# Layer-norm stage of a fused attention and channel-mix kernel: loads, normalisation and stores in another order, with fewer buffers elsewhere

## What is computed

```python
z   = layernorm(x)                       # over the last axis, eps 1e-5
q, k, v = z @ Wq, z @ Wk, z @ Wv         # 1024 -> 64 each
att = softmax(q @ k.T, axis=1)           # over the queries, not the keys
x1  = x + tile(att @ v, 16)              # 64 columns repeated 16 times
z1  = layernorm(x1)
prev = shift z1 down by one row (first row zero)
xr  = mu_r * z1 + (1 - mu_r) * prev
xk  = mu_k * z1 + (1 - mu_k) * prev
y   = x1 + sigmoid(xr @ W_r.T) * (square(relu(xk @ W_k.T)) @ W_v.T)
```

## Time and profile before

| | us |
|---|---|
| median of 2 runs | 758.27 (753.13 and 763.42) |
| the profiled execution, its own time | 766.0 |
| its span, first to last instruction on its slowest core (core 3) | 764.4 |
| spans of the 8 cores in it | 749.7 to 764.4 |

### The profile page before, as it was taken

The page is one execution under the profiler, slowest core; times in us unless marked ns, Lnnn a source line. Parts: engine busy times, 40 slices in busy tenths (PEclk is TensorE's granted clock), DMA queues, the critical chain, the costliest instruction groups (busy, mean ns, idle before and its releaser), DMA issues.

```text
span 764.4 us, 5687 instructions; the slowest of 8 cores (749.7 to 764.4 us)
## 1 busy us (share of the span) xinstructions
PE 356.5 (47%) x1392; PEld 125.2 (16%) x1392; DVE 310.8 (41%) x531; ACT 244.0 (32%) x420; POOL 47.7 (6%) x77
## 2 busy tenths in 40 slices
PE   0001300000995887777772000000237999999875
PEld 0000100000440111111112000000012444444332
DVE  3540532425751111111112586626891002227777
ACT  3202204004007888888870231210003233330000
POOL 2110111102000030000000010100000000001110
PEclk9999855555995556666655555555567999999998
DMA  9647575593701059920000004494200000007764
GB/s 237 191 166 110 165 206 80 204 218 116 110 1 33 8 72 170 234 90 2 1 0 1 14 27 144 158 212 87 44 0 0 1 1 0 1 1 249 236 231 165
DMA packets 77854, 76.22 MB, mean 100 GB/s; under 512 B 60189, under 2 KB 60205, under 8 KB 77758
## 3 DMA queue, kind: packets, MB, share of 16 engines
q0 software_dynamic: 13504, 32.32, 16.0%
q1 hardware_dynamic: 12606, 30.68, 12.5%
q10 hardware_dynamic: 51712, 12.85, 10.4%
HBM read 47.79 MB, written 21.76 MB: 91 GB/s over the span
## 4 chain that ended last, share of the span: by engine, by line
PE 27%; DMA 22%; DVE 18%; issue 15%; ACT 9%; ACTq 7%; DVEq 1%; SPq 1%; POOL 0%; POOLq 0%
DMA xst<-x_in 8%; PE ktp L886 7%; PE rps L844 7%; ACT p_sb L552 6%; PE dpool L492 6%; ACTq L314 5%; DMA z1T<-z1dram 4%; DMA zdram<-zst 4%; DMA y_out<-x2b 3%; DVE x1b L683 3%; DVE xk L823 2%; DVE tmp L993 2%; DVE tmp L989 2%; DVE zst L355 2%; PE dpool L473 2%
## 5 line engine op out<-in xcount | busy, mean ns | idle before, releaser
L552 ACT ACTIVATE p_sb<-dpool,negm 128x1024 bf16<-128x1024 f32 x128 | 140.6, 1124 | 22.2 <-DVE negm L517 20.7
L844 PE MATMUL rps<-wrT,xr 128*128 128x512 bf16 x256 | 60.2, 401 | 157.7 <-DVE xr L814 138.7
L492 PE MATMUL dpool<-qrep,krep 64*128 64x512 bf16 x256 | 101.0, 562 | 42.7 <-ACT p_sb L552 38.1
L392 PE MATMUL qk<-zT,wqk 128*128 128x512 bf16 x64 | 18.3, 439 | 181.6 <-DVE qrep L423 108.0
L944 PE MATMUL ops<-wvT,kaT 128*128 128x512 bf16 x256 | 59.6, 395 | 8.9 <-DVE tmp L989 7.1
L301 ACT ACTIVATE junk<-xst 128x1024 bf16<-128x1024 f32 x32 | 33.8, 1057 | 91.5 <-issue 83.8
L367 DVE TENSOR_REDUCE sums<-xst 128x1 f32<-128x1024 f32 x32 | 39.0, 1220 | 55.1 <-DMA xst<-x_in 55.0
L523 DVE TENSOR_REDUCE ell<-ellp 128x1 f32<-128x4 f32 x32 | 5.0, 157 | 134.6 <-ACT p_sb L552 134.5
L844 PEld LDWEIGHTS rps<-wrT,xr 128*128 128x128 bf16 x256 | 26.0, 102 | 191.6 <-issue 164.6
L886 PE MATMUL ktp<-xk,wkT 128*128 128x512 bf16 x256 | 55.6, 379 | 1.7 <-ACT r_sb L857 1.3
L911 DVE TENSOR_TENSOR kaT<-krl 128x512 bf16<-128x512 bf16 x32 | 13.6, 425 | 98.3 <-ACT krl L902 98.2
(11 more groups left out here) (83 smaller groups left out, 385.7 us busy)
## 6 DMA issues: line engine op xcount, KB each, us to landing
xst<-x_in SPq DMA_DIRECT2D x32, 512.0 KB, 8.6
xst<-x_in POOLq DMA_DIRECT2D x32, 512.0 KB, 6.6
zdram<-zst POOLq DMA_DIRECT2D x32, 256.0 KB, 8.7
y_out<-x2b SPq DMA_DIRECT2D x16, 512.0 KB, 3.6
z1dram<-z1b SPq DMA_DIRECT2D x16, 256.0 KB, 2.9
wrT<-wrT_in POOLq DMA_DIRECT2D x1, 2048.0 KB, 18.5
wkT<-wkT_in POOLq DMA_DIRECT2D x1, 2048.0 KB, 30.5
wvT<-wvT_in POOLq DMA_DIRECT2D x1, 2048.0 KB, 42.5
```

The source lines that it names most:

```text
L392: t.matmul(qk[buf][:, :], wqk[:, ct * 128:(ct + 1) * 128], zT[ct][:, nch * 512:(nch + 1) * 512], start=(ct == 0), stop=(ct == CT - 1), ski ...
L492: t.matmul(units[u][:, cc * 512:(cc + 1) * 512], krep[64 * a:64 * (a + 1), kt * 128:(kt + 1) * 128], qrep[64 * a:64 * (a + 1), c * 512:(c ...
L552: sc.activation(p_sb[kt % 4][:, s * 1024:(s + 1) * 1024], units[u][:, :], AF.Exp, bias=negm[:, kt:kt + 1], accum_out=ellp[:, 4 * (kt % 2) + s:
L844: ins = t.matmul(r_ps[t_ % 2][:, hh * 512:(hh + 1) * 512], xr[ct][:, t_ * 128:(t_ + 1) * 128], wrT[:, ct * C + hh * 512:ct * C + (hh + 1) ...
```

## The change

1. Stage A's order on DVE: the sums of group 0 come first; then for g = 1 to 7 the statistics and applies of group g - 1, and after them the sums of group g. A planner of its own, `plan_ln_af`, writes the counts. Stage F keeps the old one.
2. `zst` has 8 slots instead of 4. The apply of tile i waits for the store of tile i - 8, and ACT's squares are written into the same slot of `zst` that the apply fills later, so that the square of tile i too waits for the store of tile i - 8. `junk` is gone; so is `rowb`, whose three rows lie in `zst`.
3. `vs_sb` is `v_sb` (scaled in place), `krl` is gone (relu goes into `kaT` and is squared in place), `p_sb1` lies in the space that `zT` has left.
4. `z1dram` has 2080 rows instead of 2176: 15 and 16 zero rows instead of 63 and 64. The 16 transposes take 1040 rows instead of 1088, and H reads `z1T` from columns 16 and 15 instead of 64 and 63.

The diff, cut to its core:

```diff
-    z1dram = nc.dram_tensor("z1dram", [2176, C], BF16).ap()
+    z1dram = nc.dram_tensor("z1dram", [2080, C], BF16).ap()
-        zst = e(nc.sbuf_tensor("zst", [128, 4 * C], BF16))
-        junk = e(nc.sbuf_tensor("junk", [128, C], BF16))
+        zst = e(nc.sbuf_tensor("zst", [128, 8 * C], BF16))
...
+        vs_sb = v_sb
...
+        def plan_ln_af(n_tiles, sv0):
...
+            for s4 in range(4):
+                sv += 1
+                cnt[("sum", s4)] = sv
+            for g in range(1, ng + 1):
+                gm = g - 1
+                for op in ("smean", "svar", "msq", "varsub", "recip", "nmr"):
+                    sv += 1
+                    cnt[(op, gm)] = sv
+                for s4 in range(4):
+                    sv += 1
+                    cnt[("apply", 4 * gm + s4)] = sv
+                if g < ng:
+                    for s4 in range(4):
+                        sv += 1
+                        cnt[("sum", 4 * g + s4)] = sv
...
-        a_za = lambda i: 16 * (i // 4 + 1)
+        a_za = lambda i: 16 * (i // 8 + 1)
...
+                    if i >= 8:
+                        sc.wait_ge(ZAs[i % 8], a_za(i - 8))
...
-                    sc.activation(junk[:, :], xst[:, (i % 8) * C:(i % 8 + 1) * C],
+                    sc.activation(zst[:, (i % 8) * C:(i % 8 + 1) * C],
+                                  xst[:, (i % 8) * C:(i % 8 + 1) * C],
                                   AF.Square,
...
-                    for s in range(4):
-                        sc.wait_ge(ZAs[s], 16 * (2 * qtr + 2))
+                    for s in range(8):
+                        sc.wait_ge(ZAs[s], 16 * (qtr + 1))
...
-                    if i >= 4:
-                        v.wait_ge(ZAs[i % 4], a_za(i - 4))
+                    if i >= 8:
+                        v.wait_ge(ZAs[i % 8], a_za(i - 8))
...
-            for g in range(8):
+            def a_sums_emit(v, g):
...
+            a_sums_emit(v, 0)
+            for g in range(1, 8):
+                emit_ln_fin(v, g - 1, A_CNT, a_square(4 * (g - 1) + 3),
+                            a_sqrt(g - 1))
+                a_apply_emit(v, g - 1)
+                a_sums_emit(v, g)
...
-                sc.dma_start(out=z1T[ctn][:, 0:1088],
-                             in_=z1dram[0:1088, ctn * 128:(ctn + 1) * 128],
+                sc.dma_start(out=z1T[ctn][:, 0:1040],
+                             in_=z1dram[0:1040, ctn * 128:(ctn + 1) * 128],
...
-                v.tensor_scalar(xr[ct][:, :], z1T[ct][:, 64:2112],
+                v.tensor_scalar(xr[ct][:, :], z1T[ct][:, 16:2064],
...
-                    sc.activation(krl[:, tc * 512:(tc + 1) * 512],
+                    sc.activation(kaT[dt][:, tc * 512:(tc + 1) * 512],
```

More of the change, by code:

```diff
@@ L86, in build_program @@
         rowf = e(nc.sbuf_tensor("rowf", [128, C], F32))
-        rowb = e(nc.sbuf_tensor("rowb", [128, C], BF16))
         xlast = rowf[0:1, :]
         x1x = rowf[32:33, :]
-        z1x = rowb[0:1, :]
-        z1xm = rowb[32:33, :]
-        jrow = rowb[64:65, :]
+        z1x = zst[0:1, C:2 * C]
+        z1xm = zst[32:33, C:2 * C]
+        jrow = zst[64:65, C:2 * C]
         outx_row = e(nc.sbuf_tensor("outx_row", [1, D], F32))
@@ L108, in build_program @@
             nc.sbuf_tensor("v_sb", [128, KT * D], BF16),
-            nc.sbuf_tensor("vs_sb", [128, KT * D], BF16),
             nc.sbuf_tensor("p_sb0", [128, S], BF16),
-            nc.sbuf_tensor("p_sb1", [128, S], BF16),
             nc.sbuf_tensor("negm", [128, KT], F32),
@@ L116, in build_program @@
         ]
-        (qrep, krep, v_sb, vs_sb, p_sb0, p_sb1, negm, ellp, ell, rell) = opens(attn_cm)
+        (qrep, krep, v_sb, p_sb0, negm, ellp, ell, rell) = opens(attn_cm)
+        vs_sb = v_sb
         vT_sb = p_sb0
-        p_sb = [p_sb0, p_sb1]
+        p_sb = [p_sb0]
         SW = e(nc.semaphore("SW"))
@@ L447, in build_program @@
         out_tok, = opens(out_cm)
-        z1T_cm = [nc.sbuf_tensor(f"z1T{i}", [128, 2176], BF16, side="right") for i in range(CT)]
+        z1T_cm = [nc.sbuf_tensor(f"z1T{i}", [128, 2080], BF16, side="right") for i in range(CT)]
         z1T = opens(z1T_cm)
@@ L455, in build_program @@
         out_sb, outx_sb, xp_sb = opens(out2_cm)
-        cm_p23 = [nc.sbuf_tensor("p_sb2", [128, S], BF16, side="right"),
+        cm_p23 = [nc.sbuf_tensor("p_sb1", [128, S], BF16, side="right"),
+                  nc.sbuf_tensor("p_sb2", [128, S], BF16, side="right"),
                   nc.sbuf_tensor("p_sb3", [128, S], BF16, side="right")]
@@ L660, in _ @@
             sy.wait_ge(SD, sd_row63 - 16)
-            sy.dma_start(out=z1dram[63:64, :], in_=z1xm).then_inc(SD, 16)
+            sy.dma_start(out=z1dram[15:16, :], in_=z1xm).then_inc(SD, 16)
             sy.wait_ge(SV, SV_F0 + 11)
             sy.wait_ge(SD, sd_zero1 - 16)
-            sy.dma_start(out=z1dram[0:63, :],
-                         in_=bass.AP(zst, 0, [[4 * C, 63], [1, C]])).then_inc(SD, 16)
+            sy.dma_start(out=z1dram[0:15, :],
+                         in_=bass.AP(zst, 0, [[8 * C, 15], [1, C]])).then_inc(SD, 16)
             sy.wait_ge(SD, sd_zero2 - 16)
-            sy.dma_start(out=z1dram[2112:2176, :],
-                         in_=bass.AP(zst, 0, [[4 * C, 64], [1, C]])).then_inc(SD, 16)
+            sy.dma_start(out=z1dram[2064:2080, :],
+                         in_=bass.AP(zst, 0, [[8 * C, 16], [1, C]])).then_inc(SD, 16)
             for g in range(4):
@@ L672, in _ @@
                     sy.wait_ge(SV, F_CNT[("apply", t_)])
-                    sy.dma_start(out=z1dram[64 + t_ * 128:64 + (t_ + 1) * 128, :],
+                    sy.dma_start(out=z1dram[16 + t_ * 128:16 + (t_ + 1) * 128, :],
                                  in_=z1b[:, s * C:(s + 1) * C]).then_inc(ZSs[s], 16)
@@ L758, in _ @@
                         sc.wait_ge(SV, F_CNT[("svar", g - 2)])
-                    sc.activation(junk[:, :], x1b[:, (t_ % 8) * C:(t_ % 8 + 1) * C],
+                    sc.activation(zst[:, 2 * C:3 * C], x1b[:, (t_ % 8) * C:(t_ % 8 + 1) * C],
                                   AF.Square,
@@ L782, in _ @@
                 sc.wait_ge(SG_HI, 16 * ctn)
-                sc.dma_start(out=z1T[ctn][:, 1088:2176],
-                             in_=z1dram[1088:2176, ctn * 128:(ctn + 1) * 128],
+                sc.dma_start(out=z1T[ctn][:, 1040:2080],
+                             in_=z1dram[1040:2080, ctn * 128:(ctn + 1) * 128],
                              transpose=True).then_inc(SG_HI, 16)
@@ L911, in _ @@
                     v.tensor_tensor(kaT[dt][:, tc * 512:(tc + 1) * 512],
-                                    krl[:, tc * 512:(tc + 1) * 512],
-                                    krl[:, tc * 512:(tc + 1) * 512],
+                                    kaT[dt][:, tc * 512:(tc + 1) * 512],
+                                    kaT[dt][:, tc * 512:(tc + 1) * 512],
                                     ALU.mult).then_inc(SV, 1)
         closes(cm_ktp)
-        closes(krl_cm)
         closes(xk_cm)
```

24 lines of the change are left out of this document (11 added, 13 removed).

## The result

The changed kernel takes 743.7 us at the median of 11 runs; the kernel before, 762.2 at the median of 10. The ratio is 0.9754, with a 95% interval of 0.9713 to 0.9795: faster, by 18.4 us at the medians. 739 was forecast, with a range of 731 to 750. With eight more runs the median of the kernel before rose from 758.3 to 762.2, so the 19 us that were taken off it came out closer than the time itself.

A forecast was written before the change was run, and what follows sets the result against it. Stage A was taken as bound by a loop of waits, not one resource. On core 3, 13.0 + 5.5 + 5.5 - 3.3 + 1.0 = 21.7 us; 19 off the 758.3 median gave 739, range 731 to 750.

The forecast's parts named there:

- First quarter, 13.0: Stage A, core 3: group 1's applies 15.5 us earlier, but DMA work frees ACT at 58.4 instead of 71.4: 13.0 gained.
- Second and third quarter, 5.5 each: Stage A: applies 9.8 us apart instead of 16.55, 6.7 gained, 1.2 taken back for leftover loads beside stores: 5.5 each.
- the wait chain ends last: Stage A, second and third quarter: waits, not DMA work (34.0 us against 43.0 used), set the end; 6.7 gained before deduction.
- Last quarter, 3.3 lost: Stage A: group 7's sums, formerly hidden by transposes, now stand between the applies: 9.8 us instead of 6.6, 3.3 lost.
- The waits on stores, nothing: Stage A: ACT's squares waiting for the store of tile i - 8 add nothing; eight slots keep the 15.5 us whole.
- z1dram and H, 1.0: Second-round transposes, 48 rows of 1088 fewer: between nothing and 2.3 us for 16 of them, 1.0 us gain taken.
- The rest at nothing: Squares into zst, vs_sb in place, p_sb1 moved, relu and square within kaT: same instructions at other addresses, no time.
- From core 3 to the median: Whole kernel: gains of 21.7 us on core 3 and 18.0 on core 5 taken as 19 off the median.
- the slowed streams: Rival, stage A: denser loads and stores run at 209 GB/s instead of 290, gain 9.4 us, 749; chance 0.18.
- the waits go whole (731): Rival, stage A: stores land as before, leftover loads delay no transposes, gain 27.9 us, 730.4; chance 0.10.
- nothing comes (756): Rival: something later ends last in C, or ACT's squares keep applies from coming earlier; gain under 5 us; chance 0.04.
- The rival at 765: Rival, stage H: z1T's new offset or length slows 16 multiplies from 753 to 2352 ns, adding 25.6 us; chance 0.04.

The follow-up runs named there:

- the fourth experiment: Changed kernel, but the load of tile 12 and all behind it held until group 1's four stores landed, once: 746.5 us, ratio 0.975.
- The fifth experiment: Changed kernel, stage A from the second quarter on: sums of both groups ahead of the first group's statistics and applies: 743.7 us, ratio 0.9736.
- seventh experiments: Changed kernel with both groups' sums first in stage A from the second quarter on, and the new order in stage F too: 730.4 us, ratio 0.9590.
- the first experiment: Kernel before with only the new order of stage A on VectorE, zst keeping 4 slots: 750.9 us, ratio 0.9834.
- the third experiment: Kernel before with only the smaller z1dram (2080 rows, transposes of 1040 rows, z1T read from columns 16 and 15): ratio 0.9978.
- The second experiment: Changed kernel with the old order of stage A on VectorE, everything else of the change kept: 765.3 us, ratio 1.0016.
- the eighth experiment: Changed kernel, ScalarE squaring the next group before waiting for stores and issuing the transposes, in the first three quarters: 739.9 us, ratio 0.9715.
- the ninth: Changed kernel with ScalarE's next-group squares ahead of the transposes, and the new order in stage F as well: 730.1 us, ratio 0.9581.

## Why the prediction came out right, step by step

- **First quarter, 13.0.** On core 3 ACT was free at 58.2 (58.4 forecast; the 71.4 that it was taken from is the end of a stretch, ACT had been free at 70.9, so the gain was 12.7). That the transfers end this quarter is what the fourth experiment shows. How it shows up was wrong: the excess was to lengthen the transposes (a start between 40 and 44, 15 to 18 us of issue), and instead it held up the stores, by 6 us; the transposes began at 47.2 and took 11.1. The working took "the old distance from these applies to the transposes", which held for stores with fewer loads beside them. And the hit to 0.2 us is luck. The 54.3 us of full work were 50.1 in the changed kernel (0.99 x 24.0 + 0.70 x 23.2 + 0.91 x 11.1) for the same 13.2 MB, and the mean share was 0.86 and not 0.93, because of the tail; the two errors cancel. Core 3 was free at 54.6, 60.0 and 60.8 in the three other executions with this first quarter. On the mean of the cores the same working gives 57.0 (53.0 of work), and 57.9 to 59.8 was measured; the gain there was 9.5 (67.7 to 58.2), below the 11.5 used for core 5.
- **Second and third quarter, 5.5 each.** 8.9 and 8.1 on core 3, whose transposes before had been slow; 6.5 and 5.5 on the mean. The distance of the applies was forecast at 9.8 and is 9.5. But the step "the wait chain ends last" holds for the kernel before and only in part after the change: the fifth and seventh experiments cut 2.7 more out of the chain and got 0.4 to 2.3 of it. The 1.2 "taken back" was the first sign of this bound, and too small a one to act on.
- **Last quarter, 3.3 lost.** 2.95 between the applies on core 3, 3.2 on the mean (16.8 to 20.0 from ACT free to the copies). The fifth experiment gives 2.7 of it back.
- **The waits on stores, nothing.** Right for ACT. That eight slots are needed to keep the gain whole was right for the applies, which without them wait 10.45 us, and mostly wrong for the time, since the transfers end the quarter: the first experiment has C's copies 2.4 us later, within what two executions of the same stage A differ by.
- **z1dram and H, 1.0.** 0.9 in the pair of traces before and after, 0.1 in the third experiment, 0.6 to 1.1 between executions with either size. Likely right in kind, not shown.
- **The rest at nothing.** The second experiment, ratio 1.0016.
- **From core 3 to the median.** Core 3 gained 27.1, not 21.7; the mean of the cores 21.1; the medians 18.4. So the sum was 5.4 too small for the core that it was made on, mostly in the second and third quarter, and the 19, chosen between two sums, met the medians' 18.4 partly by luck. Of the signs, C's copies 19 to 22 earlier came out at 18.3 on the mean and 26.5 on core 3, and one of the first eight DMA slices stayed at 5.

Of the rivals, the slowed streams did not come to 749, though their ground was real: stores and transposes are slowed by loads beside them (16.5 us to landing, 20.1 and up to 32.5 us of issue). What they did not do is lower the rate: on core 3, 236 GB/s in the first 24 us where it was 209, and 245 up to the transposes where it was 193. That the waits go whole (731) fails in the first quarter: on the mean of the cores the applies came 15.3 us earlier and ACT was free only 9.5 earlier. That nothing comes (756) is excluded by applies 15.7 us earlier and an interval that ends at 0.9795. The rival at 765 is excluded by the 753 ns.

## What to carry to other kernels

In a loop where one engine both reduces the newest tiles and finishes the old ones, finish first: the finishing frees the slots that the next loads need, and with the reduction ahead of it every load waits for the load before it. Apply the same order wherever the pattern recurs, and ask in each place what ends last: in a thin stage the whole wait comes back (9.5 us in F), in a dense one it comes back until the DMA engines are busy throughout, and after that a further cut in the chain is worth less than it cuts (1.2 of 2.7 us, over two pairs of executions). Add up the DMA share over the stretch before and divide by the best share seen: it gave the end of the first quarter to 1 to 3 us on the mean of the cores, where the chain alone (41.3 and the old 14.06 of issue, 55.4) was 2.8 off on core 3. It is an estimate and no more: the same bytes took 54.3 us of share before and 50.1 after, and it does not see a tail in which few engines work. When an effect is as small as 2 us, look at a second execution with the same stage before it is given a cause.

## What the runs showed of the hardware that was not expected

- Stores beside a full queue of loads, both in pieces of 4 KB, got a third of the pieces: 334 against 658 in 12 us at a share of 0.99 (core 3). Four stores of 256 KB landed 16.4 us after their issue on the mean of the cores, 9.1 before the change, and 9.8 with the loads held back.
- A busy DMA stretch can end in a thin tail: in the last 6 us before the first transposes the 16 engines were 0.37 and 0.17 busy on the mean of the cores (0.15 and 0.05 on core 3), while the last store was still awaited. Its cause is open.
- Transposes beside loads take 1.7 to 2.8 times as long to issue, 20.1 and 24.2 us for eight on the mean (up to 32.5 on one core) against 11.5 alone, and hold ACT all that time.
- Eight cores with the same program part ways where transposes and loads are mixed: the first round ended between 61.6 and 84.8 us in the eighth experiment, between 53.9 and 61.7 in the changed kernel. Over executions the slowest core lies 9.8 above the mean of the eight in the eighth experiment and 9.4 in the ninth, 5.9 in the changed kernel and 6.7 before; but it is 9.0 in the first experiment too, which mixes nothing, so part of this may be chance. The mean core's gain of 7.7 us did not reach the metric, which is the slowest core.
